# Tile 6's row statistics on GpSimd and ScalarE, and other places for the logits and the up weights' low half, in a cross-attention and mixture-of-experts kernel

## The reference

```python
x = x + xattn(layernorm(x), ctx)        # 16 heads of 32, 1024 tokens, 2048 context rows
x = x + ffn(layernorm(x))               # 8 experts of 512, chosen by token

def xattn(x, cond):                     # all tokens attend to all context rows
    q, k, v = x @ Wq + bq, *(cond @ Wkv + bkv)
    q, k, v = fq_sym(q / sqrt(32)), fq_sym(k), fq_sym(v)      # 8-bit steps
    p = fq_unsigned(softmax(q @ k.T))                        # 8-bit steps
    return (p @ v) @ Wp + bp

def ffn(x):
    inh = sigmoid(x @ Wr / temperature)
    w = golden_weights(inh)             # in-zone experts, else the two nearest; normalised
    h = silu(x @ Wg[e]) * (x @ Wu[e])
    return sum over e of w[:, e] * (h @ Wd[e])
```

## Time and profile before

| | us |
|---|---|
| median of 3 runs | 755.05 |
| lowest, highest | 753.76, 755.77 |
| the profiled execution | 755.5 |
| its span (first to last instruction) | 753.7 |

### The profile page before, as it was taken

How to read it: one execution, slowest core, us unless ns; L and a number is a source line. 1 busy time by engine, 2 the same in 40 slices (tenths; PEclk the granted TensorE clock), 3 DMA queues, 4 the chain that set the end, 5 groups by cost and what they waited for, 6 DMA issues and landing times.

```text
span 753.7 us, 15964 instructions
## 1 busy us (share of the span) xinstructions
PE 629.9 (84%) x5281; PEld 326.0 (43%) x5281; DVE 578.9 (77%) x999; ACT 451.8 (60%) x538; POOL 365.3 (48%) x379
## 2 busy tenths in 40 slices
PE   5989999766777767677767778789999999999993
PEld 1434443233343434343434346355555555555551
DVE  4777698899999999999999999775637447465330
ACT  5233336588899999999999898234435334444321
POOL 3165354535557576667675744105433453344503
PEclk8999999899999999999999999899999999999997
DMA  8878766989999999999999998258797887967804
GB/s 215 233 154 186 162 140 111 154 149 187 178 173 178 208 180 210 185 209 183 202 187 198 185 202 156 77 172 214 198 247 141 233 205 177 250 147 222 146 11 56
DMA packets 330657, 132.28 MB, mean 175 GB/s; under 512 B 305140, under 2 KB 305140, under 8 KB 330616
## 3 DMA queue, kind: packets, MB, share of 16 engines
q1 hardware_dynamic: 323440, 115.53, 72.3%
q0 software_dynamic: 7168, 16.26, 10.5%
q10 hardware_dynamic: 8, 0.01, 0.0%
HBM read 44.33 MB, written 12.06 MB: 75 GB/s over the span
## 4 chain that ended last, share of the span: by engine, by line
PE 36%; issue 21%; DVE 19%; DMA 10%; SPq 5%; ACT 5%; POOL 2%; DVEq 1%; ACTq 0%; POOLq 0%
PE psum L1443 31%; DVE spare L1186 6%; DMA work<-work 5%; ACT work L885 3%; DMA keys_region<-values_region 2%; PE psum L1559 2%; DVE spare L1177 2%; SPq L332 2%; SPq L436 2%; DMA work<-in_ctx_dram 1%; DVE values_region L1037 1%; PE psum L1521 1%; PE psum L1699 1%; DVE work L1116 1%; DVE q_amax L1111 1%
## 5 line engine op out<-in xcount | busy, mean ns | idle before, releaser
L885 ACT ACTIVATE work<-spare,exp_bias 128x2048 int16<-128x2048 f32 (+1 forms) x128 | 255.4, 1996 | 35.9 <-DVE exp_bias L1195 30.7
L1186 DVE TENSOR_SCALAR_CACHE_REDUCE spare<-psum,q_step_now 128x1024 f32<-128x1024 f32 x128 | 161.8, 1267 | 0.0
L607 POOL CAST work<-work 128x2048 int16<-128x2048 uint8 x63 | 119.1, 1890 | 87.7 <-DMA work<-work 72.6
L1177 DVE TENSOR_SCALAR_CACHE_REDUCE spare<-psum,q_step_now 128x2048 f32<-128x2048 f32 x64 | 150.1, 2345 | 0.7 <-PE psum L1559 0.7
L1559 PE MATMUL psum<-keys_region,work 128*128 128x512 f16 x256 | 75.3, 396 | 51.1 <-DVE spare L1186 27.2
L710 POOL DMA_INDIRECT work<-x_rows,slot_tok x32 | 50.0, 1564 | 105.5 <-DVE slot_w L1375 72.1
L1559 PE MATMUL psum<-keys_region,bias_hl 128*128 128x512 f16 x256 | 72.3, 384 | 32.5 <-DVE spare L1186 28.5
L722 POOL DMA_INDIRECT out_dram<-keys_region,slot_tok x32 | 51.7, 1615 | 76.2 <-ACT keys_region L961 69.1
L1443 PE MATMUL psum<-work,spare 128*128 128x480 f16 (+1 forms) x396 | 79.2, 360 | 1.9 <-DVE work L1352 1.9
L1443 PE MATMUL psum<-work,keys_region 128*128 128x480 f16 x384 | 78.9, 366 | 0.0
L1521 PEld LDWEIGHTS psum<-values_region,work 128*128 128x128 f16 x2048 | 67.5, 96 | 25.1 <-DMA work<-work 13.5
(11 more groups left out here) (217 smaller groups left out, 1000.2 us busy)
## 6 DMA issues: line engine op xcount, KB each, us to landing
spare<-in_L_ffn_Wd_dram SPq DMA_DIRECT2D x8, 1024.0 KB, 15.4
spare<-in_L_ffn_Wg_dram SPq DMA_DIRECT2D x7, 1024.0 KB, 5.8
spare<-in_L_ffn_Wu_dram SPq DMA_DIRECT2D x7, 1024.0 KB, 10.2
work<-in_ctx_dram SPq DMA_DIRECT2D x3, 1024.0 KB, 6.0
work<-work SPq DMA_TRANSPOSE x185, 3.6
resid<-in_x_dram SPq DMA_DIRECT2D x2, 1024.0 KB, 8.5
x_rows<-work SPq DMA_DIRECT2D x8, 256.0 KB, 2.3
out_dram<-work SPq DMA_DIRECT2D x8, 256.0 KB, 2.5
```

Of the source, the lines that this page charges most:

```text
L607: nc.gpsimd.tensor_copy(p_T_int[h % 4 // 2], pair_bytes[h % 4 // 2]).then_inc(unpacked, 1)
L885: nc.scalar.activation(last_int[h % 2] if words and h >= H - 2 else p_int[h % 4], scores, ACT.Exp, bias=exp_bias[:, h % 4:h % 4 + 1], scal ...
L1177: nc.vector.tensor_scalar(staged[h % 4], psum[:, at:at + 4, :].rearrange("p b k -> p (b k)"), q_step_now[:, h:h + 1], None, ALU.mult, ALU.min,
L1186: nc.vector.tensor_scalar(staged[h % 4][:, 1024 * c:1024 * c + 1024], psum[:, at:at + 2, :].rearrange("p b k -> p (b k)"), q_step_now[:, h ...
```

## The change

Tile 6's root now is GpSimd's `deviation(6)`, its squares, normalisation and high half are ScalarE's, and its low half is GpSimd's `rows_low(6)`. The squares stand behind the last exponential, the normalisation behind the high half of the last attention columns, and the rounding behind the two copies of the turned attention. VectorE waits for them before it writes `x1` and `x1_norm` for tile 7. On TensorE the logits of tiles 0 to 5 stand before the values of heads 11 and 10 instead of behind them, in the place of eight unused matmuls; two more are left out between the turns and four before the count. VectorE cuts the up matrix's low half before it waits for expert 0's weights, and the second piece of the gate matrix before the last copy of turned rows. TensorE turns the third piece of rows before the first gate product.

```diff
--- before.py
+++ after.py
@@ -699,6 +699,8 @@
             with pool.Fori(2, QT - 1) as i:
                 attention_tile(i, True, True)
             attention_tile(QT - 1, True, False)
+            deviation(QT - 2)
+            rows_low(QT - 2)
 
 
             def gather(i, par):
@@ -898,7 +900,7 @@
                         take_projection(i - 1)
                     if h == 12:
                         take_attention(i, 0)
-                    if h == 13 and not first:
+                    if h == 13 and not first and following:
                         square_rows(i - 1)
 
             attention_tile(0, True, False)
@@ -912,16 +914,19 @@
                 nc.scalar.activation(g_inh[:, tiles, :], bank(LOGIT_BANKS[n])[:, tiles.start * E:tiles.stop * E].rearrange("p (t e) -> p t e", e=E),
                                      ACT.Exp, scale=r_temp[:, 0:1]).then_inc(gate_exp, 1)
 
+            square_rows(QT - 2)
             for g in range(DK):
                 act.wait_ge(probs_turned[1], g + 1)
                 nc.scalar.activation(last_T[1][:, 512 * g:512 * g + 512], bank(PROB_BANKS[1][g]), ACT.Copy, scale=SUBNORMAL).then_inc(probsT_out[1], 1)
             exp_logits(0)
             act.wait_ge(att_ready, 2 * QT)
             nc.scalar.activation(att_hl[:, 1, 0, :], att[:, 256:512], ACT.Copy).then_inc(att_hi, 1)
+            normalise_rows(QT - 2)
             for l in range(2):
                 act.wait_ge(last_turned, l + 1)
                 nc.scalar.activation(att_T[:, DK + 2 * l:DK + 2 * l + 2, :].rearrange("p k t -> p (k t)"), bank(3 + l)[:, 0:256], ACT.Copy
                                      ).then_inc(attT_out, 1)
+            cut_rows(QT - 2)
             act.wait_ge(exp_done, H * QT)
             cut_weights(0, 0, 0)
             cut_weights(0, 0, 1)
@@ -1278,18 +1283,9 @@
             dve.wait_ge(q_now_ready, 4 * QT)
             own.link(nc.vector.tensor_copy(slot_now[:, :], token[:, 2, :]))
             nc.vector.tensor_scalar(ident, column[:, :], slot_now[:, 0:1], None, ALU.is_equal).then_inc(ident_ready, 1)
-            dve.wait_ge(x1_squared, QT - 1)
-            own.link(nc.vector.tensor_scalar(var, x1_square[:, :], 1.0 / D, LN_EPS, ALU.mult, ALU.add))
-            rsqrt(own, var, y, t)
             for g in range(DK):
                 dve.wait_ge(probs_turned[0], g + 1)
                 nc.vector.tensor_scalar(last_T[0][:, 512 * g:512 * g + 512], bank(PROB_BANKS[0][g]), SUBNORMAL, None, ALU.mult).then_inc(probsT_out[0], 1)
-            nc.vector.tensor_scalar(x1_norm, x1, x1_mean[:, :], y, ALU.subtract, ALU.mult).then_inc(x1_normed, 1)
-            dve.wait_ge(x1_normed, QT - 1)
-            dve.wait_ge(x1T_in, 16 * (QT - 2))
-            dve.wait_ge(rows_stored, 16 * (QT - 2))
-            nc.vector.tensor_copy(x1_hl[:, 0, :], x1_norm).then_inc(x1_hi, 1)
-            rows_low(QT - 2)
             invert_sums(QT - 1, 1)
             divide(QT - 1, 1)
             dve.wait_ge(att_hi, 2 * QT)
@@ -1297,6 +1293,7 @@
             closeness(0)
             compare(0)
             dve.wait_ge(stored, 16 * (QT - 1))
+            dve.wait_ge(x1_normed, QT - 1)
             for half in range(2):
                 add_projection(QT - 1, half, bank(half)[:, 0:256])
                 half_statistics(QT - 1, half, own)
@@ -1305,6 +1302,7 @@
 
             own.link(nc.vector.tensor_scalar(var, ln1_mv[:, 1:2], LN_EPS, None, ALU.add))
             rsqrt(own, var, y, t)
+            dve.wait_ge(x1_cut, QT - 1)
             nc.vector.tensor_scalar(x1_norm, x1, ln1_mv[:, 0:1], y, ALU.subtract, ALU.mult).then_inc(x1_normed, 1)
             count_nearer(0)
             rows_low(QT - 1)
@@ -1345,14 +1343,15 @@
             own.link(nc.vector.tensor_tensor(g_tmp[:, :, :], g_w[:, :, :], tok_w[:, :, :, 2], ALU.subtract))
             own.link(nc.vector.tensor_copy(tok_w[:, :, :, 3], g_tmp[:, :, :]))
             nc.vector.tensor_tensor(tok_w[:, :, :, 4], g_tmp[:, :, :], tok_w[:, :, :, 3], ALU.subtract).then_inc(weights_made, 1)
+            cut_weights(0, 0, 1)
             dve.wait_ge(weights_full, 1)
             nc.vector.tensor_reduce(slot_w[0][:, :], bank(3)[:, 0:3 * DK].rearrange("p (s c) -> p s c", c=3), AX.X, ALU.add).then_inc(weights_ready, 1)
             for t in range(DK):
                 dve.wait_ge(rows_turned[1], t + 1)
                 nc.vector.tensor_copy(x_sel_T[0][:, t, DK:2 * DK, :].rearrange("p k t -> p (k t)"), bank(5 + 2 * (t % 2))
                                       ).then_inc(rows_out[1], 1)
-            cut_columns(slice(P, 2 * P)).then_inc(first_cut, 1)
-            cut_weights(0, 0, 1)
+                if t == 2:
+                    cut_columns(slice(P, 2 * P)).then_inc(first_cut, 1)
             cut_columns(slice(2 * P, D)).then_inc(w_ready[0], 1)
             cut_weights(0, 0, 2)
 
@@ -1624,15 +1623,14 @@
                     turn(bank(b), last_bits[n][:, 512 * g:512 * g + 512], probs_turned[n])
 
             pe.wait_ge(att_taken, 2 * QT - 1)
-            keep_busy(6, 8)
+            pe.wait_ge(x1T_in, 16 * (QT - 2))
+            logits(0)
             for h in (H, H + 1):
                 values(QT - 1, h - (7 if h % 2 else 5), True)
-            pe.wait_ge(x1T_in, 16 * (QT - 2))
-            logits(0)
             pe.wait_ge(scores_taken, 2 * H * QT)
             pe.wait_ge(ident_ready, 1)
             turn_probs(0)
-            keep_busy(4, 4)
+            keep_busy(4, 2)
             turn_probs(1)
             for h in (H + 2, H + 3):
                 values(QT - 1, h - (7 if h % 2 else 5), True)
@@ -1650,7 +1648,7 @@
             pe.wait_ge(x1_cut, QT)
             turn(bank(X1_BANKS[1]), x1_hl[:, 1, :], last_turned)
             logits(1)
-            keep_busy(2, 10)
+            keep_busy(2, 6)
 
             pe.wait_ge(mask_ready, 2)
 
@@ -1724,8 +1722,8 @@
                 if first:
                     pe.wait_ge(first_cut, 1)
                     rows_taken(2)
+                    turn_rows(2)
                     gate_product(0, 0)
-                    turn_rows(2)
                     turn_rows(3)
                     rows_taken(DK)
                     gate_product(0, 1).then_inc(gate_full, 1)
```

## The result

| | us |
|---|---|
| before, median of 11 runs (lowest, highest) | 755.02 (751.4, 755.77) |
| changed, median of 11 runs (lowest, highest) | 756.86 (754.72, 759.79) |
| ratio of changed to before, 95% interval | 1.0040, 1.0026 to 1.0054 |
| profiled execution of the changed kernel, and its span | 756.98, 755.2 |

The changed kernel is slower, by 3.0 us as the ratio puts it (2.0 to 4.1), where 0.2 us faster was forecast; the medians alone differ by 1.8 us. 756.86 lies just inside the range of 752.6 to 757.0, which is luck: the median before times the ratio is 758.0.

A forecast was written before the change was run, and what follows sets the result against it. The chain of waits up to expert 0's slot list was taken to bound what the change is worth, experts then running back to back. Terms +0.3 - 0.9 + 0.4 + 0.0 = -0.2 us gave a median of 754.8; range 752.6 to 757.0.

The forecast's parts named there:

- part 3: Up weights' low half cut beside the four gathers, before the first gate product: 0.0 us, between -0.75 and +1.4.
- rival D: Cut beside the gathers costs more than it frees: second gather held too, +1.4, or cut waits, +0.9; chance 0.12.
- rival E: TensorE's clock falls in the last attention tile and is still low at the second projection: +2.5, 757.5 us; chance 0.1.
- Part 1: Tile 6's statistics moved to GpSimd and ScalarE, behind the last exponential: +0.3 us, from 0.0 plus GpSimd and VectorE blocking.
- The exponential's 0.20 us: With tile 6's squares gone from between exponentials 13 and 14, exponential 14 starts 0.20 us sooner.
- The wait for tile 6's store: Before tile 7's cut, ScalarE may overwrite x1_hl only once the store lands: margin 0.2 us, cost 0, at most 0.5.
- Part 2: TensorE's logits moved and fillers left out: -0.9 us for four fewer before the count, +0.4 for a low clock.
- The +0.4 for a low clock in the list: List groups with fillers at the low clock take 0.33 us against 0.27, 7 times: +0.4, between 0 and 0.7.
- The rows' own arrival hides that: The twelve fillers after the list also run slow, but the gathered rows' arrival hides it.
- Part 3's trade: VectorE's 2.28 us leave the stretch before the first gate product's use; the third gather is held +0.98 us: net 0.0.
- B: Gathers beside the cut are not held and the clock recovers before the list: -1.35 us, 753.7; chance 0.2.
- C: GpSimd's chain for tile 6's statistics is shorter than in tile 5: -3.2 us with B's terms, 751.8; chance 0.13.

The follow-up runs named there:

- e2: Kernel before with only VectorE's cut of the up weights' low half moved ahead of the wait for expert 0's weights; 756.76 us, ratio to before 1.0023.
- e1: Changed kernel with the up weights' low half cut back behind the last row copy; 754.48 us, ratio to before 0.9998.
- e3: Changed kernel with one more VectorE wait, for its own last write of the weights, ahead of the up weights' cut; 754.20 us, ratio to before 0.9978.
- e12: Changed kernel profiled once more, unaltered; 757.29 us (one execution).
- e4: Changed kernel with more TensorE fillers: twelve instead of three before piece 1 of the gathered rows, five more before piece 2; 757.14 us, ratio to before 1.0023.
- e15: Kernel before profiled once more, unaltered; 753.24 us (one execution).
- e13: e3 measured a second time: changed kernel with VectorE's extra wait ahead of the up weights' cut; 755.74 us, ratio to before 1.0007.
- e14: e3 with tile 6's 256 KB store ahead of its transpose on SyncE's queue; 754.03 us, ratio to before 0.9996.
- e5: Changed kernel with the up weights' low half cut in four instructions of a quarter each at the same place; 754.89 us (one execution).
- e6: e1 with an unused VectorE maximum over the up weights, one SBUF input, in the moved cut's place; 757.74 us (one execution).
- e10: Changed kernel with e3's wait and seven fillers instead of twelve between list and weights; 754.65 us, ratio to before 1.0003.
- e8: Changed kernel with the low-half cut in four pieces: two behind VectorE's last weights write, one behind each of two row copies; 756.06 us, ratio to before 1.0008.
- e9: Changed kernel with e3's wait and ten fillers instead of six ahead of the count; 754.99 us, ratio to before 1.0006.
- e7: Kernel before with only the new place of tile 6's statistics; 755.75 us (one execution).

## Why the prediction was wrong

**The step that failed** is in part 3: "Here the cut runs 488.35 to 490.62. The second gather begins at 488.26 and is spared". I let the cut start near the end of VectorE's last write (0.05 ahead of 488.40). In the changed kernel it started 0.15 us behind the *start* of that write, 0.19 before its end (484.31 against 484.16 + 0.34), because nothing waits between the two. That turned a lead of 0.09 us into a lag of 0.04, and the second gather was held: 3.09 us for 0.95. Against the slot numbers its end came 2.1 us later (31.43 - 25.55 = 5.88, before 30.17 - 26.42 = 3.75). This is the first half of rival D, priced +1.4; D as a whole had a chance of 0.12. e2, e1 and e3 show it as the cause.

**The term was also mis-sized.** Part 3 stood at 0.0, at most +1.4. From the slot numbers to the list of expert 1 the changed kernel's profile has 26.30 us and the one before 20.83, so it measured +5.5 (e12: +5.6). In e2 it was +3.1. To the hold comes TensorE's clock, which I had only in rival E and at another place: in the changed kernel's profiles 1.2 us in the half gate product and 2.0 in the 48 matmuls. e4, where they run at full clock, has the list 2.6 us sooner in its profile. How often the clock falls in the timed runs is open; the medians of e4 and of the changed kernel do not tell the two apart.

**Part 1** was right in mechanism and near in size. The exponential's 0.20 us was 0.15 at most: exponential 14 starts 0.12 us behind the end of GpSimd's cast in the changed kernel, 0.27 behind in the kernel before, but 0.12 behind in e15, where the squares are still ahead of it and nothing is gained. Against the first profile of the kernel before I take off 0.15 below, against e15 nothing. The normalisation does take what VectorE gives (copies end at 9.08 - 0.15 = 8.93 against 8.84, or at 9.08 against 9.02; forecast 0.0 plus 0.3). I missed that the first additions were held before by VectorE's gate arithmetic and not by TensorE: they come 0.5 us sooner (10.46 to 10.09 - 0.15). The wait for tile 6's store that I put at 0, at most 0.5, took 0.5 of it back. Sum about -0.1, forecast +0.3.

**Part 2**: the count starts 1.1 us sooner (22.34 to 21.41 - 0.15; against e15, with 22.05, 0.6), forecast 0.6. The +0.4 for a low clock in the list did not come in the changed kernel (slot numbers 4.14 us behind the count, 4.08 before) and came in e4 (4.48) and in e13 (4.47). The twelve fillers did run slow (3.89 us for 2.75), as I had it, but e15, the kernel before, has 4.20 there, so the change need not be the reason. "The rows' own arrival hides that" held in the changed kernel: the first turn comes 3.68 us behind the first gather's start, before 3.66. It was wrong where they took longer: 4.68 us of fillers in e13 and e14, and a first turn at 4.33 and 4.34.

**Part 3's trade** itself, VectorE's 2.28 us against a held third gather, came out nearly as drawn once the order was as I had assumed it. e3's list is at 46.61, e13's at 47.58, before 47.25 and 46.80. From the slot numbers it is 21.1 to 21.2 us, before 20.7 to 20.8: the term is +0.3 to +0.5, not 0.0, and takes back part of what part 2 gives.

**Rivals.** B and C did not occur. D did. E's clock did fall in the last tile (0.50 from 453 to 459 in the changed kernel), and it was back at the second projection, so it cost nothing there.

## What to carry to other kernels

Before moving a long VectorE instruction with two SBUF inputs into a gap, look at what GpSimd starts in that gap: an indirect DMA that started under it was held to 0.8 or 0.9 us past its end here. If two starts lie within a few tenths of a microsecond, take the follower's start from the *start* of the instruction ahead and treat the order as unknown, or fix it with a wait, or cut the long instruction in pieces (e5: 1.49 us for 3.09). And where a step feeds TensorE, add the price of its idle time at the lower clock to the delay.

## What the runs showed of the hardware that I had not expected

- A VectorE instruction of 2.28 us with one SBUF input holds no gather (0.96 and 0.94 us beside it, e6); one with two holds the gather that starts 0.04 us behind it (3.09, changed kernel) and spares the one that started 0.18 ahead (0.96, e3). The gather in progress does not hold the cut either: 2.29 us in e3, 2.28 where it runs alone in the kernel before.
- A VectorE instruction of 0.34 us without a wait behind it overlaps the next one by 0.19 us (L1345 and L1166, changed kernel).
- TensorE's clock in this tail differs between profiles of nearly the same code: with the gathers spared, the half gate product took 1.39 us in e1, e3, e10, e13 and e14, and 2.5 to 2.6 in e6, e8 and e9. With it and with the next point, the list of expert 1 moved between 46.6 and 48.9 us in these profiles.
- In e1, e6, e7 and e8 VectorE's sum of the weights began 2.0 to 2.7 us after both VectorE and the weights' matmuls were done, and ScalarE's first row copy 0.1 behind it; both went on 0.7 to 0.8 us behind the end of the fourth gather. In the other profiles that wait is under 0.1 us. The kernel before (0.04, in both profiles) and e7 have the same code there. What releases the two engines is open; no run tests it.
